# One looped TensorE program for 28 of the 32 groups, uniform window tiles, and a second stage prepared earlier

## The chip, the cores and the metric

The kernel runs on one core of one Trainium2 chip. The metric is the device time of that core in microseconds. Before the change it is 869.58 us (median of 3 runs, 869.11 to 869.75). Lower is better.

## The reference

A batch of 16 sequences with 512 tokens of 256 channels goes through two layers, each with a residual sum and a layer norm. FFT products of twice the length, cut at 512, are causal convolutions along the tokens.

```python
q = einsum('blh,dh->bdl', u, Wq) + bq ; k, v likewise          # 256 -> 256
k  = causal_conv(k_kernel, k) + k_D * k                         # one kernel of 512 taps per channel
kv = k * v
y  = (causal_conv(ssm_kernel, kv) + D * kv) * q
x  = layernorm(u + y @ Wo.T + bo)
h  = square(relu(x @ W_fc.T))                                   # 256 -> 1024
y2 = h @ W_proj.T                                               # 1024 -> 256
# five steps: mem = 0.9*mem + y2 - (mem > 1); count += mem > 1
x  = layernorm(x + count / 5)
```

## The kernel before

Every operand of TensorE is split into a high and a low 16-bit part, and three of the four products are kept, so that the sums come out nearly as in 32 bits. That is why there are so many splits: a "hi" part is a copy to 16 bits by ScalarE, a "lo" part a subtraction by GpSimd or VectorE.

**First stage (about 48 to 404 us of the span).** The 256 channels are 8 chunks of 32, and each chunk is 4 groups of 8 channels: 32 groups, numbered 0 to 31. A projection of the chunk after next is done in four quarters (four sequences each), one quarter per group. In group g TensorE does `project` (96 matmuls, for group g + 4), `conv1` of group g (96 matmuls, keys times Toeplitz windows of the first kernel) and `conv2` of group g - 1 (96 matmuls). For groups 28 to 31 there is nothing left to project. A projection fills four PSUM banks (`PA`), and the next may begin when VectorE has read them (`proj_read`).

VectorE in group g: reads the projection (keys, values, queries: L1043, L1046, L1046), multiplies conv1's result with the values (`times_v`, L1124), multiplies conv2's result of group g - 1 with the queries (`times_q`, L1130), masks and widens the second kernel's windows of g (`windows2`, L1069 and L1089), and masks the first kernel's windows of g + 2 (`windows1`, L1069; in the last four groups it also makes one of the two shifted copies, L1076). ScalarE makes the hi parts of kv and of the next group's keys (L526, L512) and widens windows (L517, L522). GpSimd makes the two lo parts (L652, L647). The chain to the next conv1 is therefore times_v, hi of kv and keys, lo of kv, lo of keys.

The windows come by DMA from a DRAM copy of the kernels, `kpad_dram`, through the queue of SyncE: 1 MB for conv1 and 0.5 MB for conv2 of each group, and up to group 23 also two `spread` DMAs that fill `kpad_dram` eight groups ahead. The tiles for conv2 lie in four different places (`slot_of`: BASE, QUERY in the tail of the queries' tile, then TOKENS and LATE), because the keys and values of two chunks are kept at once.

TensorE's program is written out for groups 0 to 2, then a loop of nine passes with two groups each runs groups 3 to 20 (L810 to L827; an If picks the code for the projection's quarter, so that a pass holds 768 matmuls and executes 576), and groups 21 to 31 are written out again. A matmul is two instructions, a weight load and the product.

**Second stage (about 436 us to the end).** For each of 16 sequences: out projection (L855), sum and layer norm, transposes (L836), up projection (L874), relu, square, split, down projection (L881), spike counts, second norm.

**Between them.** The weights of the second layer are loaded, their largest values found (L975), reduced over partitions by GpSimd (L668), and both weights are split: hi by ScalarE (L600, L601), lo by VectorE (L1183, L1186). The first sequence's y is gathered by ScalarE (L597), turned, projected out, summed (L1214), its moments taken (L1195, L1200), the root by GpSimd (L691, L694), the shift (L1206), the norm (L554), turned and split (L560, L1220), and then the first up projection can start. GpSimd meanwhile adds the bias to u (`add_bo`, L681) and gathers y of the next sequences (`gather`, L676).

## Time and profile before

| What | us |
|---|---|
| Median of 3 runs | 869.58 |
| The profiled execution: its time | 871.54 |
| Its span | 869.4 |
| TensorE busy | 744.9 |
| VectorE busy | 703.2 |
| ScalarE busy | 529.6 |
| GpSimd busy | 391.1 |
| Mean granted TensorE clock, share of full speed | 0.95 |

The profiled execution is 1.96 us above the median of the runs, and 2.1 us of it lie outside the span. A busy share over the whole span says little here: the kernel has five stretches with different limits, which the rows below keep apart. "Idle before, issue" means that an engine waited for nothing that the profile shows.

### The profile page before, as it was taken

The page shows a single profiled execution, that of the slowest core. Times are in us where ns is not written, and L with a number is a line of the kernel's source. Part 1 is how long each engine was busy: PE and PEld are TensorE (multiplying, and loading weights), DVE is VectorE, ACT ScalarE, POOL GpSimd, SP SyncE. Part 2 cuts the span into 40 slices and gives each one's busy share as a digit, 9 for nine tenths or more (in the row PEclk, how much of TensorE's full clock was granted, in tenths as well). Part 3 has the DMA queues.
Part 4 walks back from the last instruction along what each step waited for, and adds up shares of the span by engine and source line. Part 5 has one row for each costly group of instructions (what it writes and reads, how often), then busy time and mean ns, then how long its engine had stood idle before and what let it go on. Part 6 is the DMA issues. An engine that isn't in the chain of part 4 may idle for free.

```text
span 869.4 us, 26708 instructions
## 1 busy us (share of the span) xinstructions
PE 744.9 (86%) x11392; PEld 547.4 (63%) x11392; DVE 703.2 (81%) x1100; ACT 529.6 (61%) x625; POOL 391.1 (45%) x307
## 2 busy tenths in 40 slices
PE   0068879999999798775499999999999999999993
PEld 0068879999999798775355555555555455555541
DVE  6896737877878757675569999999999999999885
ACT  2383748878877757665255556665556655566661
POOL 0332212223222212221475667866668766687542
PEclk9999969999999989776699999999999999999997
DMA  9994859999999867773000110011110111101001
GB/s 336 342 245 127 198 136 215 223 232 230 221 240 229 193 156 150 156 191 99 25 25 1 49 48 25 24 48 48 48 48 0 48 48 48 48 3 47 25 25 48
DMA packets 55580, 101.01 MB, mean 116 GB/s; under 512 B 5729, under 2 KB 41441, under 8 KB 53601
## 3 DMA queue, kind: packets, MB, share of 16 engines
q1 hardware_dynamic: 54144, 97.94, 43.9%
q10 hardware_dynamic: 1376, 2.23, 0.7%
q8 instruction: 44, 0.72, 0.4%
q14 instruction: 16, 0.12, 0.1%
HBM read 89.92 MB, written 27.01 MB: 134 GB/s over the span
## 4 chain that ended last, share of the span: by engine, by line
PE 44%; DVE 21%; POOL 17%; issue 11%; ACT 4%; DMA 1%; SPq 0%; POOLq 0%; DVEq 0%; ACTq 0%
PE ps L763 18%; POOL arena L687 14%; PE ps L741 13%; DVE arena L1238 7%; PE ps L874 5%; PE ps L881 5%; DVE u_maxima L975 2%; DVE arena L1195 2%; DVE arena L1235 2%; PE ps L855 2%; DVE arena L1214 2%; DVE arena L1220 2%; ACT arena L506 1%; PE ps L836 1%; DVE arena L1206 1%
## 5 line engine op out<-in xcount | busy, mean ns | idle before, releaser
L741 PE MATMUL ps<-arena 128*128 128x96 f16 x3072 | 143.3, 210 | 62.8 <-DVE arena L1028 51.1
L687 POOL TENSOR_TENSOR arena<-arena 128x512 f16<-128x512 f32 x128 | 178.6, 1426 | 14.9 <-ACT arena L570 14.3
L741 PEld LDWEIGHTS ps<-arena 128*128 128x128 f16 x3072 | 138.4, 100 | 64.7 <-issue 58.7
L881 PE MATMUL ps<-arena 128*128 128x512 f16 x768 | 173.2, 379 | 2.7 <-POOL arena L687 2.7
L874 PE MATMUL ps<-arena 128*128 128x512 f16 x768 | 170.8, 379 | 0.9 <-issue 0.9
L763 PE MATMUL ps<-arena 128*128 128x64 f16 (+2 forms) x5088 | 148.8, 184 | 25.9 <-issue 13.3
L763 PEld LDWEIGHTS ps<-arena 128*128 128x128 f16 x5088 | 145.4, 99 | 27.8 <-issue 20.7
L652 POOL TENSOR_TENSOR arena<-arena 128x512 f16<-128x512 f32 x32 | 37.8, 1182 | 245.3 <-ACT arena L526 245.3
L1227 DVE TENSOR_TENSOR arena<-arena 128x512 f32<-128x512 f32 x128 | 138.4, 1136 | 9.6 <-POOL arena L687 7.8
L566 ACT ACTIVATE arena<-ps,read_factor 128x512 f32<-128x512 f32 x128 | 88.0, 687 | 79.4 <-PE ps L874 62.7
L881 PEld LDWEIGHTS ps<-arena 128*128 128x128 f16 x768 | 73.9, 98 | 90.4 <-POOL arena L687 9.5
L874 PEld LDWEIGHTS ps<-arena 128*128 128x128 f16 x768 | 74.4, 98 | 86.9 <-issue 1.4
L1238 DVE SCALAR_TENSOR_TENSOR arena<-ps,stair_at,arena 128x512 bf16<-128x512 f32 x128 | 96.1, 751 | 4.5
L517 ACT ACTIVATE arena<-arena 64x1792 f32<-64x1792 f32 x60 | 98.7, 1688 | 0.8
L570 ACT ACTIVATE arena<-arena 128x512 f16<-128x512 f32 x128 | 79.3, 623 | 29.3 <-DVE arena L1227 28.2
L554 ACT ACTIVATE arena<-arena 128x256 f32<-128x256 f32 x128 | 66.2, 589 | 40.0 <-DVE arena L1206 39.4
L522 ACT ACTIVATE arena<-arena 64x1792 f32<-64x1792 f32 x42 | 69.3, 1689 | 20.8 <-DVE arena L1089 20.8
L691 POOL TENSOR_TENSOR arena<-arena,eps 128x4 f32<-128x4 f32 x32 | 11.7, 364 | 141.0 <-DVE arena L1200 141.0
L1130 DVE SCALAR_TENSOR_TENSOR qy<-ps,read_factor,qy 128x512 f32<-128x512 f32 x32 | 24.0, 751 | 57.4 <-PE ps L763 57.4
L855 PE MATMUL ps<-arena 128*128 128x256 f32 x256 | 61.6, 396 | 1.2 <-ACT arena L547 1.2
L526 ACT ACTIVATE arena<-arena 128x512 f16<-128x512 f32 x32 | 20.2, 630 | 65.7 <-DVE arena L1124 65.7
L855 PEld LDWEIGHTS ps<-arena 128*128 128x128 f32 x256 | 51.2, 201 | 10.5 <-issue 1.6
(108 smaller groups left out, 901.1 us busy)
## 6 DMA issues: line engine op xcount, KB each, us to landing
arena<-kpad_dram SPq DMA_DIRECT2D x166, 256.0 KB, 5.3
kpad_dram<-ksplit_dram SPq DMA_DIRECT2D x64, 256.0 KB, 6.1
qy<-in_uT SPq DMA_DIRECT2D x8, 1024.0 KB, 17.4
arena<-in_u SPq DMA_DIRECT2D x16, 512.0 KB, 4.1
out<-arena SPq DMA_DIRECT2D x16, 512.0 KB, 3.0
qy<-kpad_dram SPq DMA_DIRECT2D x22, 256.0 KB, 6.5
arena<-in_k SPq DMA_DIRECT2D x2, 512.0 KB, 4.8
ksplit_dram<-arena ACTq DMA_DIRECT2D x2, 512.0 KB, 3.3
```

The lines of the kernel that those rows point to most:

```text
L517: nc.scalar.activation(*as_pairs(*shifted(windows1_of(s, half))), ACT.Copy).then_inc(c1_copied, 1)
L522: nc.scalar.activation(*as_pairs(*widened(windows2_of(g, half), HP)), ACT.Copy).then_inc(c2_copied, 1)
L566: nc.scalar.activation(relu_h[:, f], PH[:, f % 2], ACT.Relu, scale=read_factor[:, 4:5]).then_inc(relu_ready, 1)
L570: nc.scalar.activation(h16[:, 0, f], h_square[:, f % 4], ACT.Copy).then_inc(h_hi, 1)
L687: nc.gpsimd.tensor_tensor(h16[:, 1, f], h_square[:, f % 4], h16[:, 0, f], ALU.subtract).then_inc(h_lo, 1)
L741: last = nc.tensor.matmul(o, u16[:, x, t, tok:tok + P], wcur[:, w, t], start=(k == 0), stop=(k == 3 * DT - 1))
L763: last = nc.tensor.matmul(out[:, ch * COL + delta * B:(ch + 1) * COL], win[:, delta * P:(delta + 1) * P], data(xp, ch)[:, 0:cols], start=( ...
L855: last = nc.tensor.matmul(PW[:, j // 2, (j % 2) * D:(j % 2 + 1) * D], yT[:, t, j * P:(j + 1) * P], wo[:, t], start=(t == 0), stop=(t == DT ...
L874: last = nc.tensor.matmul(PH[:, f % 2], wf16[:, w, t, f * P:(f + 1) * P], x16[:, r, x, t], start=(k == 0), stop=(k == 3 * DT - 1))
L881: return nc.tensor.matmul(PD[:, t], wp16[:, w, f, t * P:(t + 1) * P], h16[:, h, f], start=first, stop=last)
L1227: nc.vector.tensor_tensor(h_square[:, f % 4], relu_h[:, f], relu_h[:, f], ALU.mult).then_inc(square_ready, 1)
L1238: ins = nc.vector.scalar_tensor_tensor(c, y, stair_at[:, n:n + 1], c, ALU.is_gt, ALU.add)
```

## The change

1. Keys, values and windows. The keys' and values' tiles hold one chunk instead of two: a quarter of the next chunk is written into the place that the group just used leaves free. For that the layout alternates, so that for every second chunk keys and values are read out of PSUM in four pieces of 128 columns each and not in one of 512 (`read_scaled`). The values are now read behind times_v of the same group, and with a wait for it. kv has a tile of its own. The keys' 16-bit tile has one buffer. The eight window tiles are one array `T`; all loads of conv2's windows wait for the group two before.
2. TensorE's program is written out for groups 0 to 3 and loops over groups 4 to 31 in 14 passes. A second If leaves out the projection in the last two passes.
3. End of the first stage. The second layer's weights are loaded one group earlier, u without waiting for conv2; times_q of group 30 goes behind windows2 of group 31.
4. Start of the second stage. GpSimd does both add_bo first, then both gathers, then the first root. VectorE's split of the second weight goes behind the first sequence's statistics. TensorE projects out sequence 1 before it turns x of sequence 0.

```diff
-        kbuf = part(16, F32, "p (r q n) -> p r q n", r=2, q=GPC)
-        vbuf = part(16, F32, "p (r n) -> p r n", r=2)
+        kbuf = part(8, F32, "p (a b n) -> p a b n", a=GPC, b=GPC)
+        vbuf = part(8, F32, "p (a b n) -> p a b n", a=GPC, b=GPC)
+        kv = part(2, F32)
...
-        k16 = part(4, F16, "p (r a n) -> p r a n", r=2, a=2)
+        k16 = part(2, F16, "p (a n) -> p a n", a=2)
...
-            LOOPED = range(3, QUERY_UNTIL + 1)
-            for g in range(LOOPED.start):
-                step(g)
-            with pe.Fori(0, len(LOOPED) // 2) as nth:
-                pair_of_steps(LOOPED.start, nth)
-            for g in range(LOOPED.stop, NG):
-                step(g)
+            FIRST = GPC
+            for g in range(FIRST):
+                step(g)
+            with pe.Fori(0, (NG - FIRST) // 2) as nth:
+                pair_of_steps(nth)
...
+            def read_scaled(s, buf, quarter, r, chunk, banks):
+
+                src, factor, bias_s = tiles_of(banks, s), read_factor[:, 2 * s:2 * s + 1], bias_of(chunk, s)
+                if r == 0:
+                    return nc.vector.scalar_tensor_tensor(buf[:, quarter].rearrange("p b (d m) -> p (b d) m", d=G),
+                                                          src, factor, bias_s, ALU.mult, ALU.add)
+                for n in range(GPC):
+                    some = slice(n * G, (n + 1) * G)
+                    last = nc.vector.scalar_tensor_tensor(buf[:, n, quarter].rearrange("p (d m) -> p d m", d=G),
+                                                          src[:, some], factor, bias_s[:, some], ALU.mult, ALU.add)
+                return last
...
                 if more:
-                    if s % GPC == 0 and not (first and s == 0):
-
-                        dve.wait_ge(kv_lo, g)
-                    read_projection(s % GPC, (s // GPC + 1) % 2, g + GPC, chunk + s // GPC + 1)
+                    dve.wait_ge(k_lo, g + 1)
+                    read_keys_queries(s % GPC, (s // GPC + 1) % 2, g + GPC, chunk + s // GPC + 1)
                 times_v(s, g, base + (s // GPC + 1) * GPC)
-                if g:
+                if more:
+                    dve.wait_ge(kv_ready, g + 1)
+                    read_values(s % GPC, (s // GPC + 1) % 2, chunk + s // GPC + 1)
+                if g and not (isinstance(g, int) and g == NG - 1):
                     times_q((s - 1) % PAIR, g - 1)
...
             add_bo(0, 0, 1)
+            add_bo(1, 1, 1)
             pool.wait_ge(y_ready, NG)
-            pool.wait_ge(y_seq_ready, 1)
             gather(1, 1)
+            gather(2, 0)
             root(0, 0)
-            add_bo(1, 1, 1)
-            gather(2, 0)
...
             turn_y(1, 1)
+            project_out(1)
             turn_x(0, 0)
-            pe.wait_ge(f_lo, 2)
-            pe.wait_ge(f_hi, 2)
+            pe.wait_ge(f_lo, 1)
+            pe.wait_ge(f_hi, 1)
```

VectorE in group 0, the pattern of every group of an even chunk, before: the projection is read in three instructions, then comes times_v (L1124), then windows2. Names in brackets are the semaphores that an instruction waits for.

```order
L1043 SCALAR_TENSOR_TENSOR arena<-ps,read_factor,arena 128x512 [waits proj]
L1046 TENSOR_TENSOR arena<-ps,arena 128x128x4
L1046 TENSOR_TENSOR qy<-ps,arena 128x128x4
L1124 SCALAR_TENSOR_TENSOR arena<-ps,read_factor,arena 128x512 [waits proj_read,c1_half]
L1069 TENSOR_TENSOR arena<-arena 32x8x32 [waits t2_in0]
```

The same place now, with times_v at L1076:

```order
L989 SCALAR_TENSOR_TENSOR arena<-ps,read_factor,arena 128x128 [waits proj,k_lo]
L989 SCALAR_TENSOR_TENSOR arena<-ps,read_factor,arena 128x128 x3
L998 TENSOR_TENSOR qy<-ps,arena 128x128x4
L1076 TENSOR_TENSOR arena<-ps,arena 128x4x32x4 [waits proj_read,c1_half]
L989 SCALAR_TENSOR_TENSOR arena<-ps,read_factor,arena 128x128 [waits kv_ready]
L989 SCALAR_TENSOR_TENSOR arena<-ps,read_factor,arena 128x128 x3
L1025 TENSOR_TENSOR arena<-arena 32x8x32 [waits t2_in0,t2_zero]
```

The values' reading has moved from ahead of times_v to behind it, so the projection's banks come free only after conv1, and nine instructions stand where there were three.

VectorE at the end of the first stage before, from the widening of group 30's windows on (L975 is the largest value of a weight, L1130 times_q):

```order
L1089 COPY arena<-arena 32x8x480 [waits c2_masked] x2
L975 TENSOR_REDUCE part_max<-arena 128x1 [waits ld_wf]
L1124 SCALAR_TENSOR_TENSOR arena<-ps,read_factor,arena 128x512 [waits proj_read,c1_half,vlink]
L1130 SCALAR_TENSOR_TENSOR qy<-ps,read_factor,qy 128x512 [waits c2_half]
L1069 TENSOR_TENSOR arena<-arena 32x8x32 [waits t2_in0]
L1069 TENSOR_TENSOR arena<-arena 32x8x32 [waits t2_in1]
```

The same place now (L917 is the largest value, L1083 times_q, L1025 and L1043 masks and widening):

```order
L1043 COPY arena<-arena 32x8x480 [waits c2_masked] x2
L917 TENSOR_REDUCE part_max<-arena 128x1 [waits ld_wf]
L1076 TENSOR_TENSOR arena<-ps,arena 128x4x32x4 [waits proj_read,kv_lo,c1_half,vlink]
L1025 TENSOR_TENSOR arena<-arena 32x8x32 [waits t2_in2]
L1025 TENSOR_TENSOR arena<-arena 32x8x32 [waits t2_in3]
L1043 COPY arena<-arena 32x8x480 [waits c2_masked] x2
L1083 SCALAR_TENSOR_TENSOR qy<-ps,read_factor,qy 128x512 [waits c2_half]
```

times_q of group 30 has moved behind the masks and the widening of group 31.

GpSimd between the stages before, from the reduction over partitions on (L681 is add_bo, L676 gather, L691 and L694 the root):

```order
L668 ISA all_max<-part_max 128x3 [waits part_max2_done]
L681 ISA
L681 TENSOR_TENSOR arena<-arena 128x1024 [waits ld_u_seq0,ld_wo]
L676 COPY arena<-qy 128x1024 [waits y_seq_ready,y_ready]
L691 TENSOR_TENSOR arena<-arena,eps 128x4 [waits moments1_ready]
L694 TENSOR_TENSOR arena<-arena,half_neg 128x4 [waits var_eps_ready0]
L681 TENSOR_TENSOR arena<-arena 128x1024 [waits ld_u_seq1]
L676 COPY arena<-qy 128x1024 [waits y_turned]
```

And now:

```order
L611 ISA all_max<-part_max 128x3 [waits part_max2_done]
L624 ISA
L624 TENSOR_TENSOR arena<-arena 128x1024 [waits ld_u_seq0,ld_wo]
L624 TENSOR_TENSOR arena<-arena 128x1024 [waits ld_u_seq1]
L619 COPY arena<-qy 128x1024 [waits y_ready]
L619 COPY arena<-qy 128x1024 [waits y_turned]
L634 TENSOR_TENSOR arena<-arena,eps 128x4 [waits moments1_ready]
L637 TENSOR_TENSOR arena<-arena,half_neg 128x4 [waits var_eps_ready0]
```

The second add_bo and the second gather now stand ahead of the first root.

## Rows read from the trace of the kernel before

**Rows 1.** Busy time by stretch: length, then each engine (instructions), clock, DMA share, GB/s.
```profile
101.60:131.30 29.70, 22.30 (x582) 21.74 (x577) 14.44 (x24) 16.31 (x13) 5.66 (x6) 0.77 0.66 151
131.30:279.30 148.00, 146.62 (x4609) 145.99 (x4610) 116.94 (x180) 120.78 (x94) 36.34 (x31) 1.00 0.99 227
279.30:359.10 79.80, 69.74 (x2021) 68.44 (x2017) 54.21 (x82) 55.91 (x45) 17.79 (x15) 0.94 0.72 161
359.10:403.90 44.80, 29.49 (x865) 28.52 (x864) 33.05 (x44) 26.75 (x21) 9.76 (x9) 0.70 0.75 188
...
435.50:869.40 433.90, 415.71 (x2121) 225.12 (x2119) 389.43 (x644) 250.02 (x409) 282.53 (x217) 0.99 0.11 35
```

**Rows 2.** Timeline of TensorE, groups 21 and 22: start, length, line, instructions, idle before.
```profile
287.83 2.28 PE L763 MATMUL ps<-arena 128*128 128x64 f16 x82 [1.44 <-issue]
289.96 2.12 PE L741 MATMUL ps<-arena 128*128 128x96 f16 x46
292.94 2.29 PE L741 MATMUL ps<-arena 128*128 128x96 f16 x50 [0.86 <-issue]
```

**Rows 3.** DMA queues in the looped stretch 131.3 to 279.3 us: packets, MB, share.
```profile
q14 instruction: 4, 0.03, 0.1%
```

**Rows 4.** DMA queues in the written-out stretch 279.3 to 359.1 us.
```profile
q8 instruction: 15, 0.25, 1.4%
```

**Rows 5.** Timeline of VectorE in one looped group.
```profile
210.05 0.74 DVE L1043 SCALAR_TENSOR_TENSOR arena<-ps,read_factor,arena 128x512 f32<-128x512 f32 x1
...
212.31 0.75 DVE L1124 SCALAR_TENSOR_TENSOR arena<-ps,read_factor,arena 128x512 f32<-128x512 f32 x1 [0.34 <-PE ps L763]
214.82 0.75 DVE L1130 SCALAR_TENSOR_TENSOR qy<-ps,read_factor,qy 128x512 f32<-128x512 f32 x1 [1.75 <-PE ps L763]
```

**Rows 6.** Timeline of all engines, same group: the next projection, and GpSimd's lo part.
```profile
213.81 1.16 POOL L652 TENSOR_TENSOR arena<-arena 128x512 f16<-128x512 f32 x1 [7.11 <-ACT arena L526]
...
214.64 4.24 PE L741 MATMUL ps<-arena 128*128 128x96 f16 x96
```

**Rows 7.** Timeline of VectorE near the start: a 256-column instruction.
```profile
42.65 0.35 DVE L1021 TENSOR_SCALAR arena<-arena,d_scale 128x256 f32<-128x256 f32 x1
```

**Rows 8.** Timeline of TensorE, group 1: the wait ahead of its convolutions.
```profile
85.91 5.17 PE L763 MATMUL ps<-arena 128*128 128x64 f16 x192 [1.48 <-POOL arena L647]
```

**Rows 9.** Timeline of all engines, groups 28 to 31.
```profile
367.64 6.58 PE L763 MATMUL ps<-arena 128*128 128x32 f16 x185 [3.28 <-issue]
...
371.06 0.75 DVE L1130 SCALAR_TENSOR_TENSOR qy<-ps,read_factor,qy 128x512 f32<-128x512 f32 x1 [4.05 <-PE ps L763]
...
372.23 2.22 DVE L1089 COPY arena<-arena 32x3840 f16<-32x3840 f16 x2
...
373.41 3.29 ACT L522 ACTIVATE arena<-arena 64x1792 f32<-64x1792 f32 x2 [3.50 <-DVE arena L1089]
...
391.13 2.29 DVE L975 TENSOR_REDUCE part_max<-arena 128x1 f32<-128x2048 f32 x1
...
394.95 1.16 POOL L652 TENSOR_TENSOR arena<-arena 128x512 f16<-128x512 f32 x1 [6.44 <-ACT arena L526]
```

**Rows 10.** Timeline of all engines, between the stages.
```profile
403.90 0.38 POOL L668 PARTITION_ALL_REDUCE all_max<-part_max  x1 [7.80 <-issue]
...
411.11 2.34 POOL L681 TENSOR_TENSOR arena<-arena 128x1024 f32<-128x1024 f32 x1 [6.83 <-issue]
...
423.96 2.31 DVE L1206 SCALAR_TENSOR_TENSOR arena<-arena 128x4 f32<-128x4 f32 x1 [1.46 <-POOL arena L694]
426.19 1.92 POOL L676 COPY arena<-qy 128x1024 f32<-128x1024 f32 x1
...
428.43 1.97 PE L836 MATMUL ps<-ident,arena 128*128 128x128 f32 x8 [9.93 <-ACT arena L554]
430.19 5.51 PE L855 MATMUL ps<-arena 128*128 128x256 f32 x16
...
435.54 10.52 PE L874 MATMUL ps<-arena 128*128 128x512 f16 x48
```

More of the change, by code:

```diff
@@ L415, in _ @@
                     spread(s + AHEAD)
-                second = [(g, half) for g in range(1, NG) for half in range(2) if loaded_at(g, half) == s]
-                for g, half in second:
-                    if not use_before(g, half) and slot_of(g, half)[0] != LATE:
-                        load_windows2(g, half)
                 if s + 2 < NG:
@@ L783, in conv1 @@
                     pe.wait_ge(kv_ready, g - 1)
-                convolve(0, PC1[:, s % 2], lambda a, ch: k16[:, s % 2, a, ch * COL:(ch + 1) * COL],
-                         lambda half, c, a: windows1_of(s, half)[:, c, a], g + 1, c1_half)
+                for half in range(2):
+                    pe.wait_ge(c1_copied[half], g + 1)
+                    convolve(half, PC1[:, s % 2], k16, lambda c, a: windows1_of(s, half)[:, c, a], c1_half)
             def conv2(s, g):
@@ L914, in body @@
             def body(i, r, left):
-                if left:
+                if left and not (isinstance(i, int) and i == 0):
                     project_out(i + 1)
@@ L1050, in read_projection, with read_values @@
+            def read_values(quarter, r, chunk, banks=PA):
+                read_scaled(1, vbuf, quarter, r, chunk, banks).then_inc(proj_read, 1)
                 if quarter == GPC - 1 and chunk + 1 < NC:
@@ L1053, in read_projection @@
                     nc.vector.tensor_copy(wcur, wnext).then_inc(wcur_ready, 2)
+            def read_projection(quarter, r, n, chunk, banks=PA):
+                read_keys_queries(quarter, r, n, chunk, banks)
+                read_values(quarter, r, chunk, banks)
             def mask(conv, s, g, half):
@@ L1059, in mask @@
                 else:
-                    place, nth = slot_of(g, half)
-                    times = USES[place, nth].index((g, half)) + 1
-                    dve.wait_ge(t2_in[2 * place + nth], 16 * times * (PIECES if place == TOKENS else 1))
+                    dve.wait_ge(t2_in[s % 2 * 2 + half], 8 * (g - s % 2) + 16)
                 if conv:
```

295 lines of the change are left out of this document (121 added, 174 removed).

## Prediction

> **What bounds the kernel now.** I read the busy time by stretch first, because the page's shares over the whole span mix five stretches [rows 1]. From 435.5 us on TensorE is busy for 415.7 of 433.9 us and the granted clock is 0.99: the second stage is one long TensorE stretch that the change leaves alone. Whatever makes it start earlier is handed to the end in full. From 131.3 to 279.3 us TensorE is busy for 146.6 of 148.0 us at full clock. These are 16 looped groups, 9.25 us each. TensorE is the bound, and VectorE with 116.9 us has 1.9 us of air in a group. From 279.3 to 359.1 us the same 288 matmuls a group take 79.8 / 7 = 11.4 us, though VectorE and the DMA queues are less busy than before (DMA share 0.72 against 0.99). So no engine's work is the bound there.
>
> The timeline of TensorE shows what is: gaps that nothing in the profile releases, put down to "issue". One lies ahead of 287.83, the next ahead of 292.94, and between them stand 82 + 46 = 128 matmuls [rows 2], which are 256 instructions. The same distance returns all along the written-out groups. The DMA queues say why this is code: in the written-out stretch the queue marked instruction moved 15 packets with 0.25 MB [rows 4], 16.7 KB a packet, and 7 x 288 matmuls make 15.75 pieces of 128: one packet for each 128 matmuls. In the looped stretch there is no row of that queue at all; what is marked instruction there is another queue with 0.03 MB [rows 3]. A loop body that is in place is not loaded again; straight code is loaded block by block and TensorE waits at block boundaries. The first pass of the loop, 101.6 to 131.3 us, took 29.7 us for the work of 18.5, at clock 0.77 [rows 1]. That is the price of loading a body.
>
> The Trainium skill, "Runtime: NRT & Kernel Launch", section "Instruction fetch mechanics", has two rules on this. It says that crossing a 16 KiB boundary is mostly hidden; the trace disagrees, with 1.44 and 0.86 us in front of two neighbouring blocks [rows 2]. By that rule the written-out groups would gain nothing from a loop. It also says that a taken branch out of the two-page window forces a fetch and that kernels prefer to be unrolled; the eight passes of rows 1 and 3 speak against it here. Both are rivals below, with times worked out from rows.
>
> **The change, part by part.** All sums are on the profiled execution, 871.54 us, which is 1.96 above the median of the runs.
>
> Start, group 0. The values are now read behind times_v, so the projection of group 1 waits for conv1 of group 0, then times_v (0.75) and the values. In even chunks these are four pieces of 128 columns. No row shows such a piece; it lies between a quarter of the 0.74 us of the 512-column one [rows 5], 0.19 us, and the 0.35 us of a 256-column instruction [rows 7]. I take 0.30, nearer to the second, whose width is the nearer one, and keep 0.35 for the bound. So 0.75 + 0.1 for the wait + 1.2 = 2.05 us later. Of this 1.48 was waited for GpSimd anyway, ahead of conv1 of group 1 [rows 8]. The rest with the later key chain: **+0.8**.
>
> Groups 4 to 27, VectorE in the looped group. Before, reading starts at 210.05 and times_v at 212.31 with 0.34 us idle; then VectorE idles 1.75 us until conv2 is done, and TensorE starts the next projection at 214.64 [rows 5, 6]. Now keys (4 x 0.30) and queries (at most 0.74) end at 212.0, times_v still runs from 212.31 to 213.06, the values end at 213.06 + 0.1 + 1.2 = 214.4. That is 0.25 us before TensorE wants the banks. At 0.35 a piece it is 214.56, still in time; the cover is the 1.75 us of idle time, and it is then used up. If a piece costs 0.45 each of the 16 groups with pieces (12 of them looped) waits some 0.35 us. I take **0**, and +5 as the end of the bound. The one key buffer costs nothing: hi of the keys is made behind times_v, thus behind conv1 in any case. SyncE's loads keep the order that groups 1 to 19 have now, and there the DMA share is 0.99 and TensorE does not wait.
>
> The Trainium skill, "VectorE: DVE Perf Modes", section "The TRN2 errata", gives a fixed price per instruction and advises tiles of 512 elements or more, against this change. By its formula of 58 to 120 cycles beside 128 columns a piece is an estimated 0.19 to 0.26 us; no run here shows one yet, and with it the sum stays at 0.
>
> Group 3 is written out now, at 11.4 instead of 9.25 us: **+2.1**. The loop's first pass moves from groups 3 and 4 to 4 and 5 and costs what it cost.
>
> Groups 21 to 27 at the looped pace: 79.8 - 7 x 9.25 = **-15.0**. So group 27 ends at 359.1 - 15.0 + 2.9 = 347.0.
>
> Groups 28 to 31, 359.1 to 403.9. Here a cycle runs over three engines: times_q at 371.06, masks, widening from 372.23 (half of 2.22 for the first half of the channels), ScalarE's two copies (3.29), and the second half of conv2, about a quarter of the 6.58 us for two convolutions at low clock [rows 9]: 1.17 + 1.11 + 3.29 + 1.65 with 0.4 for hand-overs = 7.6 us from times_q to times_q. Group 28 took 12.0 (359.1 to 371.06) because of a code stall of 3.28 us ahead of 367.64 and the copies behind it. New: times_q of 27, 28 and 29 come 7.8 us apart, 23.4 us after the start. Then 0.75, masks and widening 3.2, the largest value 2.29 [rows 9], times_v of group 31 with 0.75, and kv's lo part ends 1.91 us after times_v does (213.06 to 213.81 + 1.16 [rows 5, 6]): 32.3 us, with some tenths for the low clock 32.6. Before it ended at 396.11, that is 37.0 us after the start. **-4.4**. times_q of group 31 then follows some 5 us later instead of 7.8, but it isn't what is late next.
>
> Between the stages GpSimd is. Its reduction needs a code load: it starts 7.80 us after kv's lo part, and add_bo another 7.2 us after that, at 411.11, with 6.83 us idle [rows 10]. That is 15.0 us behind kv's lo part, and I keep it. Before, root of sequence 0 ended when the shift began, 423.96, 27.85 behind it. The shift waited for VectorE's second split. Now that split stands behind the shift, and GpSimd does 2 x 2.34 (add_bo) + 2 x 1.92 (gather without VectorE's split beside it [rows 10]) and then the root, 0.2 + 1.1: 15.0 + 4.7 + 3.9 + 1.3 = 24.9. **-2.9**. The two splits' order alone would have given 4; GpSimd's order takes a part of it back. The shift took 2.31 us beside GpSimd's add_bo for 4 columns; now nothing runs beside it, 0.2: **-2.1**. The moved split (up to 4 us, beside a busy GpSimd) lies under norm, transposes and hi part.
>
> From the end of the norm to the first up projection: 428.4 to 435.54 is 7.1 us, with transposes, hi and lo part, and the out projection of sequence 1, 5.51 us at low clock, in front [rows 10]. Now it waits only for the out projection that began before (0 to 2 us), then transposes 1.0 to 2.0, hi 1.0, lo 1.2: 3.4 to 6.4. I take 5.0: **-2.1**.
>
> Sum: 0.8 + 0 + 2.1 - 15.0 - 4.4 - 2.9 - 2.1 - 2.1 = -23.6. Profiled 847.9, median **846.0 us**.
>
> **Rivals.**
>
> A, the values' reading becomes TensorE's wait. For it: 0.25 us of cover. Against it: the bound of 0.35 us a piece. With +5 us: 851.
>
> B, the gain between the stages is eaten, because GpSimd's code load, its two add_bo and a slower clock set the first root. 7.1 us of the sum go: 853.
>
> C, the gaps aren't loading of code (the first rule above) but go with the state of the end, for instance its tiles' loads. Then groups 21 to 27 keep their 11.4 us: 846.0 + 15.0 = 861. Against it: the 128-matmul distance.
>
> D, slower: the second rule above, as a mechanism here. The body no longer stays in place, because a second If is added, and each pass loads it. The first pass shows the price, 29.7 - 18.5 = 11.2 us; 13 further passes make +146 us and the time 992. It decides when the body exceeds what is kept: now it is again 768 matmuls with a few compare instructions more. Eight passes of the old body cost nothing, so the margin must be smaller than those few instructions.
>
> **How the numbers follow.** The forecast 0.74, A 0.09, B 0.09, C 0.04, D 0.04. Its own range is 841 to 851: clock and hand-overs in groups 28 to 31 and between the stages are worth some 4 us to each side. The range for 8 in 10 reaches over A and B and to a tail in which the clock rises: 839 to 856. A measurement of this kernel can tell 0.2%, 1.7 us, from no change. Faster 0.95 (forecast, A, B, C and a rest), same 0.01, slower 0.04.
>
> **What would show it.** TensorE's groups 4 to 27 in pairs of 18.5 us from the second pass on, without packets in the second instruction queue; 29 to 30 us for the first pass. No idle time of TensorE released by VectorE's reading. Group 27's end near 347 us, kv's lo part of group 31 near 379.5, the root near 404.5, the first up projection near 412, and from there 434 us to the end. The forecast is wrong if the passes are longer than 18.7 us, if pieces take over 0.35 us, or if the first up projection starts after 418.

## The result

| | median us | runs | range |
|---|---|---|---|
| before, beside it | 869.66 | 4 | 869.11 to 871.72 |
| changed | 859.80 | 4 | 858.63 to 861.3 |

The ratio is 0.9878, 95% interval 0.9852 to 0.9903: 9.9 us faster, where the forecast had 23.6 and a range of 839 to 856. The sign was right and the size was not. The profiled execution took 861.3 us, its span is 859.3. Measured once more beside the later experiments, the changed kernel gave 860.62 (858.76 to 861.44, 4 runs, 868.91 for the kernel before), with a second profile.

### The profile page after: what moved, and what is told of

Its sections match the earlier page's. It is cut to its first block, busy times and chain, and to the rows that moved or that the text cites. A ratio compares the mean times of both kernels' runs of the same rounds, so it can differ in the third digit from the quotient of the medians.

```text
span 859.3 us, 26944 instructions
## 1 busy us (share of the span) xinstructions
PE 743.8 (87%) x11392; PEld 545.7 (64%) x11392; DVE 713.3 (83%) x1192; ACT 529.9 (62%) x625; POOL 390.3 (45%) x307
## 4 chain that ended last, share of the span: by engine, by line
PE 44%; DVE 24%; POOL 17%; issue 10%; DMA 2%; ACT 1%; SPq 0%; POOLq 0%; DVEq 0%; ACTq 0%
PE ps L697 16%; PE ps L683 15%; POOL arena L630 14%; DVE arena L1184 7%; PE ps L813 5%; PE ps L820 5%; DVE u_maxima L917 2%; DVE arena L1181 2%; PE ps L794 2%; DVE arena L1141 2%; DVE arena L1166 2%; DVE arena L1160 2%; DVE arena L971 1%; DMA arena<-kpad_dram 1%; PE ps L772 1%
## 5 line engine op out<-in xcount | busy, mean ns | idle before, releaser
L697 PE MATMUL ps<-arena 128*128 128x64 f16 (+3 forms) x6144 | 172.2, 182 | 23.3 <-issue 8.9
L697 PEld LDWEIGHTS ps<-arena 128*128 128x128 f16 x6144 | 169.7, 97 | 24.5 <-issue 14.7
L683 PEld LDWEIGHTS ps<-arena 128*128 128x128 f16 x3072 | 138.4, 101 | 64.6 <-issue 56.4
L820 PEld LDWEIGHTS ps<-arena 128*128 128x128 f16 x768 | 74.0, 98 | 90.6 <-POOL arena L630 9.7
L813 PEld LDWEIGHTS ps<-arena 128*128 128x128 f16 x768 | 74.3, 98 | 89.5 <-issue 4.0
L467 ACT ACTIVATE arena<-arena 64x1792 f32<-64x1792 f32 x64 | 105.1, 1687 | 14.7 <-DVE arena L1043 14.7
L462 ACT ACTIVATE arena<-arena 64x1792 f32<-64x1792 f32 x60 | 98.7, 1689 | 0.8
L514 ACT ACTIVATE arena<-arena 128x512 f16<-128x512 f32 x128 | 79.3, 623 | 29.4 <-DVE arena L1173 28.4
L1043 DVE COPY arena<-arena 32x3840 f16<-32x3840 f16 x64 | 72.9, 1177 | 1.0
L1025 DVE TENSOR_TENSOR arena<-arena 64x512 f16<-64x512 f16 (+1 forms) x128 | 58.3, 482 | 10.6 <-DMA arena<-kpad_dram 9.6
L794 PE MATMUL ps<-arena 128*128 128x256 f32 x256 | 64.0, 407 | 2.3 <-ACT arena L491 2.3
L794 PEld LDWEIGHTS ps<-arena 128*128 128x128 f32 x256 | 52.7, 207 | 12.6 <-issue 1.6
```

Of the source, the lines that this page charges most:

```text
L462: nc.scalar.activation(*as_pairs(*shifted(windows1_of(s, half))), ACT.Copy).then_inc(c1_copied[half], 1)
L467: nc.scalar.activation(*as_pairs(*widened(windows2_of(g, half), HP)), ACT.Copy).then_inc(c2_copied, 1)
L514: nc.scalar.activation(h16[:, 0, f], h_square[:, f % 4], ACT.Copy).then_inc(h_hi, 1)
L683: last = nc.tensor.matmul(o, u16[:, x, t, tok:tok + P], wcur[:, w, t], start=(k == 0), stop=(k == 3 * DT - 1))
L697: last = nc.tensor.matmul(out[:, ch * COL + delta * B:(ch + 1) * COL], taps(c, tp)[:, delta * P:(delta + 1) * P], data[:, xp, ch * COL:ch ...
L794: last = nc.tensor.matmul(PW[:, j // 2, (j % 2) * D:(j % 2 + 1) * D], yT[:, t, j * P:(j + 1) * P], wo[:, t], start=(t == 0), stop=(t == DT ...
```

## The profile after

Busy time by stretch of the changed kernel, with the columns of [rows 1]: group 3; the first pass of the loop; the eleven passes over groups 6 to 27; groups 28 to 31; between the stages; second stage.
```profile
104.00:116.00 12.00, 11.09 (x295) 10.73 (x291) 8.74 (x19) 7.21 (x7) 2.42 (x3) 0.87 0.73 164
116.00:146.80 30.80, 21.58 (x577) 21.13 (x577) 14.37 (x23) 16.38 (x13) 5.25 (x5) 0.83 0.66 150
146.80:354.20 207.40, 202.78 (x6336) 201.26 (x6336) 173.96 (x320) 168.06 (x131) 51.27 (x44) 1.00 0.94 213
354.20:395.60 41.40, 27.05 (x865) 26.37 (x864) 35.69 (x43) 28.03 (x22) 11.23 (x9) 0.86 0.82 199
395.60:425.25 29.65, 18.12 (x56) 14.25 (x57) 11.91 (x30) 10.85 (x10) 11.19 (x7) 0.62 0.06 18
425.25:859.30 434.05, 415.62 (x2120) 225.11 (x2120) 388.55 (x644) 250.07 (x409) 283.05 (x217) 0.99 0.11 35
```
The second stage is what it was, 434.05 against 433.9 us. Everything lies in when it starts: 425.25 against 435.54 before and about 412 forecast. The seven groups that took 11.4 us each now run at the loop's pace, and the queue that had 15 packets there [rows 4] is gone from the whole looped stretch; only the other instruction queue is left:
```profile
q1 hardware_dynamic: 19425, 44.15, 94.2%
q14 instruction: 5, 0.04, 0.1%
```
But a pass takes 207.4 / 11 = 18.85 us, not 18.5 (from the first projection of one pass to that of the next it is 18.89 over the ten passes from 146.79 to 335.71). In TensorE's timeline (columns as in [rows 2]) the first projections of four successive passes stand behind gaps, three of them released by nothing and one by VectorE's copy of the chunk's weights (L1007):
```profile
165.74 4.25 PE L683 MATMUL ps<-arena 128*128 128x96 f16 x96 [0.43 <-issue]
...
184.60 4.25 PE L683 MATMUL ps<-arena 128*128 128x96 f16 x96 [0.50 <-issue]
...
203.53 1.66 PE L683 MATMUL ps<-arena 128*128 128x96 f16 x35 [0.42 <-DVE arena L1007]
...
222.36 4.25 PE L683 MATMUL ps<-arena 128*128 128x96 f16 x96 [0.46 <-issue]
```
VectorE in the same kernel, near the end of the loop and in groups 29 and 30: two pieces of 128 columns (L989) take 0.60 us, 0.30 each as forecast. In group 29 VectorE waits 2.06 us for windows from memory, and its widening for group 30 takes 3.18 us instead of 2.22:
```profile
353.74 0.60 DVE L989 SCALAR_TENSOR_TENSOR arena<-ps,read_factor,arena 128x128 f32<-128x128 f32 x2
...
375.34 0.42 DVE L1025 TENSOR_TENSOR arena<-arena 64x512 f16<-64x512 f16 x1
377.82 0.42 DVE L1025 TENSOR_TENSOR arena<-arena 64x512 f16<-64x512 f16 x1 [2.06 <-DMA arena<-kpad_dram]
...
382.15 3.18 DVE L1043 COPY arena<-arena 32x3840 f16<-32x3840 f16 x2
```
Between the stages, TensorE and then GpSimd. The out projection of sequence 1 (the second L794) starts at 415.24, behind GpSimd's gather, and holds the transposes of x until 421.75, though ScalarE's norm had begun at 415.54 and ended at 417.62:
```profile
412.15 1.97 PE L772 MATMUL ps<-ident,arena 128*128 128x128 f32 x8 [3.90 <-POOL arena L619]
415.24 6.68 PE L794 MATMUL ps<-arena 128*128 128x256 f32 x16 [1.11 <-ACT arena L491]
421.75 1.04 PE L772 MATMUL ps<-ident,arena 128*128 128x128 f32 x8
425.25 7.07 PE L813 MATMUL ps<-arena 128*128 128x512 f16 x32 [2.46 <-DVE arena L1166]
```
```profile
396.90 0.39 POOL L611 PARTITION_ALL_REDUCE all_max<-part_max  x1 [5.94 <-issue]
404.43 5.81 POOL L624 TENSOR_TENSOR arena<-arena 128x1024 f32<-128x1024 f32 x2 [7.15 <-issue]
410.20 3.81 POOL L619 COPY arena<-qy 128x1024 f32<-128x1024 f32 x2
413.98 0.19 POOL L634 TENSOR_TENSOR arena<-arena,eps 128x4 f32<-128x4 f32 x1
414.25 1.06 POOL L637 TENSOR_TENSOR arena<-arena,half_neg 128x4 f32<-128x4 f32 x1
```

## The experiments

All start from the changed kernel. The kernel before was measured beside every group of them and had medians of 868.91 to 870.25 us. Single profiles are compared by what happens inside them. The start of the first stage alone shifts a whole profile by up to 3 us: with the same code ahead of it, group 3 starts at 101.80 where the granted clock from 72 us on was 0.94, and at 104.92 where it was 0.84.

### Is it the loading of code?

Groups 4 to 31 written out.
```
-            with pe.Fori(0, (NG - FIRST) // 2) as nth:
-                pair_of_steps(nth)
+            for g in range(FIRST, NG):
+                step(g)
```


> The changed kernel with TensorE's groups 4 to 31 written out, no loop and no branch. Theory (code is loaded block by block and TensorE waits at block boundaries): no pace of 9.25 us anywhere, groups 6 to 27 at about 11.4 us each instead of the 9.44 of the changed kernel, so group 27 ends some 43 us later, near 397 us of the span, about 150 packets of 16 KB in the second instruction queue over the first stage, total near 895 to 905 us. Rival (the gaps belong to the state at the stage's end, not to code): groups at 9.25 us, since the branches are gone too, total near 855 us.

Measured: 898.97 us (one run), 39 us more than the loop. The written-out program's instruction queue over the whole span:
```profile
q8 instruction: 79, 1.29, 0.7%
```
against 25 packets and 0.41 MB in the changed kernel. That is half of the 150 packets that had been expected, a miscount: 28 groups of 288 matmuls make 63 pieces of 128. TensorE in one of these groups, with 81 + 47 = 128 matmuls between two gaps:
```profile
220.34 3.60 PE L683 MATMUL ps<-arena 128*128 128x96 f16 x81 [2.01 <-issue]
223.78 1.38 PE L697 MATMUL ps<-arena 128*128 128x64 f16 x47
226.65 3.49 PE L697 MATMUL ps<-arena 128*128 128x16 f16 x127 [1.50 <-issue]
```
Groups 6 to 27 take 11.3 us each (138.88 to 386.85), and group 27 ends 10 us earlier than expected. The same tile places and transfers, only TensorE's program differs, and the gaps are back all along it. So rival C of the prediction falls: the gaps are loading of code.

The Trainium skill, "Runtime: NRT & Kernel Launch", section "Instruction fetch mechanics", calls the crossing of a 16 KiB boundary mostly hidden; this run disagrees, by 39 us.

Four groups in one pass, which needs no If, in six passes, with groups 28 to 31 written out.
```
-            with pe.Fori(0, (NG - FIRST) // 2) as nth:
-                pair_of_steps(nth)
+            with pe.Fori(0, (NG - GPC - FIRST) // GPC) as nth:
+                four_steps(nth)
+            for g in range(NG - GPC, NG):
+                step(g)
```


> The changed kernel with a loop of 6 passes of four groups (groups 4 to 27) and no If at all: a pass holds 1152 matmuls instead of 768. Groups 28 to 31 are written out. Theory (a body stays in place only up to some size between 768 and 1152 matmuls, and is loaded in every pass beyond it): groups at 11 to 12 us in every pass, packets in the second instruction queue throughout, total near 900 us. Rival (any loop stays in place): four groups in 37.0 us, that is 9.25 each, no packets after the first pass, total near 856 us.

Measured: 920.5 us (one run), the slowest of all. Its queue, and the start of one of its passes:
```profile
q8 instruction: 88, 1.44, 0.7%
```
```profile
215.11 6.73 PE L683 MATMUL ps<-arena 128*128 128x96 f16 x96 [6.46 <-issue]
```
A body of 1152 matmuls is loaded again in every pass, with 4.8 to 6.5 us ahead of it and 50 to 51 us for four groups, which is worse than straight code. The body of 768 matmuls stays in place. The mechanism of rival D exists; its threshold lies between the two and the change is on the good side.

The same section of the Trainium skill says that a taken branch out of the two-page window forces a fetch. Two pages of 16 KiB are too few for the changed kernel, whose body of 768 matmuls is 6 blocks and drew no packet in eleven passes. But the section also gives TensorE a larger memory than the other engines, 128 KiB or 2048 instructions, and with that both runs agree: 1536 instructions stay, 2304 don't.

### Why 18.9 us a pass?

The outer If of each projection taken away, groups 28 to 31 written out.
```
-                with pe.If(nth < (NG - GPC - FIRST) // 2):
-                    with pe.If(nth % 2 == 0):
+                with pe.If(nth % 2 == 0):
...
-            with pe.Fori(0, (NG - FIRST) // 2) as nth:
+            with pe.Fori(0, (NG - GPC - FIRST) // 2) as nth:
                 pair_of_steps(nth)
+            for g in range(NG - GPC, NG):
+                step(g)
```


> The changed kernel with the loop over groups 4 to 27 only (12 passes) and without the second If; groups 28 to 31 are written out. Theory (each further branch of a pass costs some 0.2 us of TensorE's time): passes of 18.5 us again instead of 18.89, so the start of group 28 comes 4.3 us earlier, near 350 us; behind it the written-out groups show issue gaps again, which may take back 1 to 3 us; total near 857 us. Rival (the passes are longer because of VectorE's later reading of the values or of the transfers): passes stay at 18.9 us, the start of group 28 stays at 354 us, total 860 to 862 us.

Measured: 860.82 (859.34 to 861.93, 5 runs). The passes take 18.62 us, 0.27 less, as the theory had it, and group 28 starts near 350.7 instead of 354.2. But the last four groups, written out again, lose nearly the same (30 packets of code against 25, and 74.1 us from there to the first up projection instead of 71.05), so the time is where the rival had it.

The loop over groups 3 to 26 as in the kernel before, with one If and the uniform places.
```
-            FIRST = GPC
+            FIRST = 3
...
-            with pe.Fori(0, (NG - FIRST) // 2) as nth:
-                pair_of_steps(nth)
+            with pe.Fori(0, 12) as nth:
+                pair_of_steps(nth)
+            for g in range(FIRST + 24, NG):
+                step(g)
```


> The tile places and all engines but TensorE as changed; TensorE's program is groups 0 to 2 written out, a loop of 12 passes over groups 3 to 26 with one If ahead of each projection as in the kernel before, and groups 27 to 31 written out. Theory: the second pair of Ifs costs 0.25 us a pass in groups 4 to 27, and writing out group 3 costs 2.7 us; so passes take 18.6 us and the loop's first pass begins at 104 (not 116); the group-27 part is written out again, 2 to 3 us more, and the tail's code stalls cost what they cost in the kernel with one If (about 3 us against the loop). Group 28 starts near 352 and the time is 858 to 861. Rival: the slower passes come from VectorE's order and the smaller pieces, then passes take 18.9 us as in the changed kernel and the time is 862 to 865.

Measured: 856.19 (856.1 to 859.26, 4 runs), 2 us better than the theory had. Ten passes from 132.03 to 318.50 make 18.65 us each. Group 28 starts near 347.6, 6.6 us earlier than in the changed kernel: 2.3 of these lie ahead of group 3 (101.72 against 104.01), where both have the same code and the clock differs (0.94 against 0.89), 3.4 in groups 3 to 5 (39.4 against 42.8 us), the rest behind them, where the written-out group 27 gives some of the passes' gain back. Groups 28 to 31 and the time between the stages cost 72.5 against 71.05 us: their code stalls give back 1.5.

Two Ifs more, around the first convolutions.
```
+                with pe.If(nth < NG):
-                conv1(0, g)
+                    conv1(0, g)
```


> The changed kernel with two more Ifs in TensorE's loop body, one around conv1 of each group, whose condition always holds; no matmul is added. Theory: each If that TensorE passes at a boundary of a group costs it some 0.12 to 0.25 us of waiting that nothing releases. The passes grow from 18.89 by 0.25 to 0.5 us to 19.1 to 19.4, and the time from 859.8 by 14 x 0.25 to 14 x 0.5 to 863 to 867. Rival: the longer passes come from VectorE's smaller pieces and its order, or from the If ahead of a projection waiting for the reading: passes stay at 18.9 us and the time at 860.

Measured: 861.61 (860.88 to 862.17, 4 runs) against 860.62 for the changed kernel beside it, passes of 18.91 us against 18.90. Nothing gained on the question: a condition that always holds is dropped when the program is built, so TensorE's program has 10 unconditional jumps instead of 8 and the same 6 comparing branches. The two jumps add nothing that shows, here in front of the first convolutions.

The same around the projections.
```
+                with pe.If(nth < NG):
                     with pe.If(nth < (NG - GPC - FIRST) // 2):
```


> The changed kernel with a third If around each of the two projections of TensorE's loop body, whose condition always holds. Two more Ifs around the first convolutions left the passes at 18.9 us. Theory: what costs is an If in front of a projection, where the loop's jump and the other Ifs stand already: taking one level away gave 0.24 to 0.27 us a pass, so one more level adds as much: passes of 19.1 to 19.2 us and 863 to 864. Rival: an If costs nothing anywhere as long as the body stays in place, and the 0.25 us come from something else that went with it (how the two branches lie in the code): 18.9 us and 860.

Measured: 860.64 (859.09 to 861.01, 4 runs), passes of 18.89. For the same reason this was the changed kernel once more, with the same 8 jumps and 6 comparing branches, and it told nothing for either side.

Then with a condition that has to be compared.
```
+                with pe.If(nth < (NG - FIRST) // 2 - 1):
                     with pe.If(nth < (NG - GPC - FIRST) // 2):
```


> The changed kernel with a third If around each of the two projections, now with a condition that TensorE has to compare itself (it holds in the first 13 of 14 passes); the Ifs with a condition that always held had been dropped when the program was built, so they had added no comparison at all. Theory: a comparison with its branch in front of a projection costs TensorE 0.12 to 0.25 us each, since one level less gave 0.24 to 0.27 us a pass: passes grow from 18.89 to 19.1 to 19.4, the time to 863 to 866. Rival: the branch as such is free and the difference came with something else: passes of 18.9 us, 860.

> As the kernel with the third compared If, but only around the second projection of the body, away from the loop's jump back. Theory: both places cost the same, so passes grow by half of what both together do (19.0 to 19.15). Rival: only the place behind the loop's jump costs, then passes of 18.9 us here and all of the growth belongs to the first.

Measured: both places 863.07 (860.11 to 865.67, 5 runs), the second place alone 860.19 (2 runs). The timeline of TensorE tells more than the times. Two passes of the first:
```profile
299.25 4.25 PE L683 MATMUL ps<-arena 128*128 128x96 f16 x96 [0.63 <-issue]
308.63 4.25 PE L683 MATMUL ps<-arena 128*128 128x96 f16 x96
318.43 4.25 PE L683 MATMUL ps<-arena 128*128 128x96 f16 x96 [0.55 <-issue]
327.67 4.25 PE L683 MATMUL ps<-arena 128*128 128x96 f16 x96
337.49 4.25 PE L683 MATMUL ps<-arena 128*128 128x96 f16 x96 [0.58 <-issue]
```
and of the second:
```profile
298.69 4.25 PE L683 MATMUL ps<-arena 128*128 128x96 f16 x96 [0.46 <-issue]
308.07 4.25 PE L683 MATMUL ps<-arena 128*128 128x96 f16 x96
317.75 4.25 PE L683 MATMUL ps<-arena 128*128 128x96 f16 x96 [0.43 <-issue]
327.02 4.25 PE L683 MATMUL ps<-arena 128*128 128x96 f16 x96
336.73 4.25 PE L683 MATMUL ps<-arena 128*128 128x96 f16 x96 [0.46 <-issue]
```
From 146.04 to 337.49 are ten passes: 19.145 us each, 0.25 more. From 146.61 to 336.73: 19.01, 0.12 more. So a compared branch in front of a projection costs TensorE 0.12 us, at the second place by this run and at the first by the difference of the two, and the two Ifs that the change adds are 0.25 us of the 0.35 to 0.4 that a pass is longer.

The rest, some 0.1 us a pass, stays open. The row with L1007 above is a candidate: once in four passes TensorE waits for the copy of the weights, which now stands behind the values' reading. In the kernel looped from group 3 that wait has a price. It comes ahead of the second projection, and the pass around it takes 19.13 us where the others take 18.47 to 18.65:
```profile
187.58 4.25 PE L683 MATMUL ps<-arena 128*128 128x96 f16 x96
197.20 4.25 PE L683 MATMUL ps<-arena 128*128 128x96 f16 x96 [0.37 <-DVE arena L1007]
206.71 4.25 PE L683 MATMUL ps<-arena 128*128 128x96 f16 x96 [0.26 <-issue]
```
That is 0.5 us in four passes, 0.12 a pass. In the changed kernel the same wait adds nothing: two successive passes take 37.76 and 37.80 us with it and 37.76 to 37.81 without, since a gap of the same length stands there in any case. So rival A, that the reading and what follows it make TensorE wait, did not cost the changed kernel time, and where it shows it is about 1.5 us in 12 passes, not 5.

### Groups 28 to 31

The loads of the second stage's weights one group later each, where they were before.
```
-                if s == NG - 4:
+                if s == NG - 3:
                     sp.dma_start(wf_st, ...).then_inc(ld_wf, 16)
-                if s == NG - 3:
+                if s == NG - 2:
                     sp.dma_start(wp_st, ...).then_inc(ld_wp, 16)
```


> The changed kernel with the second layer's two weights loaded one group later, where they were before. Theory (the 1 MB load of the first weight goes ahead of group 31's windows and delays them): VectorE's wait of 2.06 us for windows ahead of times_v of group 30 is gone, kv's lo part of group 31 ends some 2 us earlier relative to the start of group 28, total 857.5 to 859 us. Rival (the windows come late anyway, or the later weight delays the largest value instead): the total does not move by more than 0.5 us, or it is slower by up to 1 us.

Measured: 858.61 (857.15 to 861.22, 4 runs). The medians of 858.61 and 859.8 (860.62 later) can't be told apart, the profiles can. VectorE in groups 29 and 30: no wait for windows, and the widening is back at 2.22:
```profile
374.14 0.75 DVE L1025 TENSOR_TENSOR arena<-arena 64x512 f16<-64x512 f16 x2
...
380.24 2.22 DVE L1043 COPY arena<-arena 32x3840 f16<-32x3840 f16 x2
```
The stretch from the start of group 28 to the first up projection is 68.35 us against 71.05, 2.7 less. Of these 1.7 lie ahead of the end of kv's lo part of group 31 (35.05 us after the start against 36.8, and 36.8 again in the second profile of the changed kernel). The rest lies between the stages, where profiles of the same code differ by as much (next section), so 1.7 is what the loads show.

### Between the stages

The out projection of sequence 1 put back behind the transposes.
```
-                if left and not (isinstance(i, int) and i == 0):
+                if left:
                     project_out(i + 1)
...
             turn_y(1, 1)
-            project_out(1)
             turn_x(0, 0)
```


> The out projection of sequence 1 is put back behind the transposes of x (before the first up projection), the rest as changed. Theory: in the changed kernel it started only at 415.24, since y of sequence 1 is gathered at the earliest behind two add_bo, and its 6.68 us at low clock held the transposes until 421.75, though the norm was done at 417.62. Put back, the transposes start at 417.7 (after the norm), hi and lo part are done by 421.1, but the projection then runs from 418.7 to 425.4 and the first up projection starts at 425.4: 0 to +0.5 us against the changed kernel, 859.8 to 860.5. The move of this projection by itself bought nothing. Rival (the forecast's view, the order of the two is worth 2.1 us): the up projection starts near 427.5 and the time is 862.

Measured: 858.48 (858.11 to 860.13, 4 runs). From the reduction (L611) to the first up projection 424.13 - 395.99 = 28.1 us against 28.35. Moving it bought nothing. The spread of this stretch is worth knowing: the ten other profiles whose code between the stages is that of the changed kernel have 26.9 to 28.3, most of them 27.8 or more.

GpSimd's order.
```
             add_bo(0, 0, 1)
-            add_bo(1, 1, 1)
             pool.wait_ge(y_ready, NG)
             gather(1, 1)
-            gather(2, 0)
+            add_bo(1, 1, 1)
             root(0, 0)
+            gather(2, 0)
```


> GpSimd does add_bo(0), gather(1), add_bo(1), root(0), gather(2) in place of add_bo(0), add_bo(1), gather(1), gather(2), root(0). Theory: what holds the first up projection back is the start of the out projection of sequence 1, and that waits for gather(1). gather(1) now ends near 409.3 instead of 412.1, the out projection runs from 412.4 to 419.1, the root ends at 413.4, the norm near 416, the transposes start at 419.1 and the first up projection near 422.5: 2.7 us earlier than 425.25, 857.1. Rival: the norm or the splits set the start and the order of GpSimd is worth nothing: 859.8.

Measured: 857.14 (855.33 to 859.0, 4 runs), as the theory had it. TensorE:
```profile
410.85 1.93 PE L772 MATMUL ps<-ident,arena 128*128 128x128 f32 x8 [2.13 <-POOL arena L619]
413.89 5.62 PE L794 MATMUL ps<-arena 128*128 128x256 f32 x16 [1.11 <-ACT arena L491]
419.35 1.04 PE L772 MATMUL ps<-ident,arena 128*128 128x128 f32 x8
422.85 9.44 PE L813 MATMUL ps<-arena 128*128 128x512 f16 x43 [2.47 <-DVE arena L1166]
```
From the reduction at 397.64 to the up projection are 25.2 us, 3.1 less than in the changed kernel. The two further kernels with this order, below, have 24.8 and 25.6, so all three lie under the whole spread of the old order, by 1.4 us at the least.

The second layer's split put back in front of the first sum.
```
+            dve.wait_ge(f_hi, 2)
+            nc.vector.scalar_tensor_tensor(wp16[:, 1], wp_st, ...).then_inc(f_lo, 1)
...
             first_sum(0, 0)
             norm_shift(0, 0)
-            dve.wait_ge(f_hi, 2)
-            nc.vector.scalar_tensor_tensor(wp16[:, 1], wp_st, ...).then_inc(f_lo, 1)
```


> VectorE's split of the second layer's weights is put back ahead of the first sum, the rest as changed. Theory: the first split ended at 405.72 and the first sum waited until 408.29 for the out projection, so the second split (2.35 us alone) fits into that idle time: the sum starts at 408.3 to 409.5 (the split runs beside GpSimd's add_bo and may take up to 4 us), GpSimd's add_bo get up to 1 us longer, and the root, which stands behind two gathers, ends 0 to 1 us later: 859.8 to 861. Rival (the forecast's view, that putting the split behind the statistics is worth 4 us of which GpSimd's order takes a part back): root and up projection come 2 to 4 us later, 862 to 864.

Measured: 861.95 (861.48 to 863.89, 4 runs). GpSimd's two add_bo and VectorE's second split:
```profile
403.84 8.14 POOL L624 TENSOR_TENSOR arena<-arena 128x1024 f32<-128x1024 f32 x2 [6.83 <-issue]
```
```profile
405.34 4.43 DVE L1135 SCALAR_TENSOR_TENSOR arena<-arena,w_scale 128x2048 f16<-128x2048 f32 x1
```
The split takes 4.43 us beside add_bo instead of 2.35, and the two add_bo 8.14 instead of 5.81. From the reduction to the up projection 29.0 us, 0.7 more. The median is 1.3 to 2.2 above the changed kernel, so the time is on the edge between the two theories; the profile speaks for the smaller price. The new place of the split was right by a small amount, and what it frees is GpSimd.

### Together

Late loads and GpSimd's order on the changed loop.

> The changed kernel with the later loads of wf and wp and GpSimd's order add_bo(0), gather(1), add_bo(1), root(0), gather(2). The loop is the changed one. If the two causes are independent: times_q of group 31 comes 2.7 us earlier after the start of group 28 and the first up projection 7.2 instead of 7.6 us behind the norm with the norm itself earlier: 859.8 - 2.7 - 2.4 = 854.7, by the medians 856.0. Rival: they share one wait, then 857.1, what the better of them has alone.

Measured: 854.59 (853.25 to 855.36, 4 runs), where the sum had 854.7 and the rival 857.1. From the start of group 28 to the first up projection are 66.7 us, against 68.35 with the late loads, 68.2 with GpSimd's order, and 71.05 and 70.65 in the two profiles of the changed kernel. So the two add up for the most part. The times alone don't prove it: as ratios to the kernel before they are 0.9834 (0.9807 to 0.9861) for both edits and 0.9841 (0.9812 to 0.987) for GpSimd's order alone.

All three: the loop over groups 3 to 26, late loads, GpSimd's order.

> Three edits on the changed kernel together: TensorE's loop over groups 3 to 26 with one If a projection and groups 27 to 31 written out, the loads of wf and wp one group later each (as in the kernel before), and GpSimd's order add_bo(0), gather(1), add_bo(1), root(0), gather(2). If the three causes add up: 859.8 - 3.6 - 1.2 - 2.7 = 852.3, by the profiles of each (-5.3, -2.7 and -2.4 at the first up projection) 849.5. Rival: in the written-out groups 27 to 31 the stalls of TensorE that nothing releases set the pace, so the later loads give nothing there: 854.

Measured: 852.95 (852.27 to 855.7, 5 runs), ratio to before 0.9823 (0.9799 to 0.9847), against 860.62 for the changed kernel beside it: 7.7 us faster. The sum of the three (852.3) and the rival (854) both lie within the range of its runs, so this doesn't decide between them, and its runs overlap with those of the two edits above. It has the lowest median found.

## Why the prediction was wrong

The end of each step, on the profiled execution of the changed kernel; the miss is 861.3 - 847.9 = 13.4 us.

| step | forecast | measured | miss |
|---|---|---|---|
| start of group 3 | 102.4 | 104.01 | +1.6 |
| groups 3 to 5 | 40.9 | 42.8 | +1.9 |
| 11 passes, groups 6 to 27 | 203.5 | 207.4 | +3.9 |
| start of 28 to kv's lo part of 31 | 32.6 | 36.8 | +4.2 |
| lo part to root | 24.9 | 24.35 | -0.6 |
| root to first up | 7.3 | 9.94 | +2.6 |

**Right.** The central reading, that the gaps are code loading at every 128 matmuls and a body in place is free of them. Rivals C and D fall with it. Also about 0.30 us a piece (the Trainium skill's formula, "VectorE: DVE Perf Modes", section "The TRN2 errata", gave an estimated 0.19 to 0.26), and the shift at 0.16 us without GpSimd beside it. Rival B, that the gain between the stages is eaten, did not come: from kv's lo part to the first up projection are 34.3 us instead of 39.4, 5.1 of the 7.1 forecast.

**Right by luck.** The stretch from kv's lo part to the root: -2.9 forecast, -3.5 measured. The forecast kept 15.0 us from kv's lo part to add_bo, on the ground that the reduction needs a code load behind the lo part. It was 13.5. The reduction waits for VectorE's last largest value (the semaphore `part_max2_done`). VectorE finds it here, before and now, and has the small product of it behind, done at 402.08 and 395.19:
```profile
399.55 2.29 DVE L975 TENSOR_REDUCE part_max<-arena 128x1 f32<-128x2048 f32 x1
```
```profile
392.67 2.27 DVE L917 TENSOR_REDUCE part_max<-arena 128x1 f32<-128x2048 f32 x1
```
The reduction starts 1.8 us behind that before, 1.7 now, and 1.5 to 2.1 in the profiles of the experiments. Before, the value came 6.0 us behind kv's lo part, now 4.2, since times_q of group 30 no longer makes VectorE wait ahead of the masks. The forecast had no term for this part of the change. Against it stand the two add_bo, 5.81 instead of 4.7 beside VectorE's first split.

**Groups 4 to 27 at 0** is the step that failed most: 3.9 us over the eleven passes and 1.1 in the first (30.8 against 29.7). It held the extra compare instructions for nothing in time and weighed them only as code size (rival D). Shown: 0.12 us for each, twice a pass, which is 2.8 of the 3.9 us; the other 1.1 and the first pass stay open. The prediction checked that the values' reading ends before TensorE wants the banks, and left out the copy of the weights that follows it on VectorE at the end of each chunk. TensorE does wait for that copy, but in the changed kernel at no price.

**Groups 28 to 31 at -4.4** gave -0.2 by kv's lo part. The model had the cycle of times_q, masks, widening, copies and conv2, 7.8 us. Measured, times_q of 27 comes 8.7 us after the stretch begins (conv1 of 28 waits 2.65 us for ScalarE's copy of its windows; in ScalarE's order that copy stands behind the keys' hi part, which waits for the values' reading), that of 28 another 7.9 and that of 29 another 9.2 (8.5 with the late loads), since windows stood behind a megabyte of weights in the queue. The change puts these loads one group earlier, and the forecast gave that no term. The late loads show 1.7 us of the miss. The 2.65 us wait was not tried alone. From times_q of 29 to the end of kv's lo part of 31 are 11.0 us instead of 9.2, mostly because the widening of group 30 took 3.18 instead of 2.22 and the lo part, which now runs beside the widening of group 31, 1.84 instead of 1.16.

**Norm to first up at 5.0** was 7.6. It gave the out projection of sequence 1, already begun, 0 to 2 us ahead of the transposes. That projection started only 2.4 us before the norm's end, because gather(1) stands behind two add_bo, took 6.68 us instead of 5.51, and held the transposes for 4.1. Both orders of TensorE cost the same (28.1 and 28.35). GpSimd's order alone gives 3.1, or 1.4 at the least by the spread above.

**Start and group 3.** The start moved 0.1 to 3.3 us in the profiles. Where TensorE's projections 0 and 1 ran at 5.85 us instead of 4.25 (granted clock 0.89 for that stretch) it is 2.4; in the kernel from group 3 on, with 4.25 for the first, group 3 starts at 101.72, 0.1 late. So this term is within the clock of a run. Group 3 written out and then the first pass cost 42.0 to 43.2 us in the profiles with the changed loop, where the loop from group 3 takes 39.4 for the same three groups: 2.6 to 3.8 against 2.1.

The range was too narrow because five of the six misses have one sign: where the rows left a choice, most terms took the better side, and the sum added these.

## What to carry to other kernels

A loop is worth having where code is loaded block by block, but its body must fit: here 768 matmuls stay in place and 1152 do not, and too large a body is worse than straight code. Branches that compare, in front of TensorE's work, are not free where TensorE is the bound (here busy for 202.78 of 207.40 us): count them. Before an idle stretch is kept as a fixed price, look up which semaphore the instruction waits for. When an engine does a row of small jobs in a gap between stages, sort them by who waits next (here gather(1) ahead of the second add_bo, some 3 us), and keep large loads behind the small ones of the current stage.

## What had not been expected of the hardware

- A compared branch ahead of a projection: 0.12 us of TensorE each; two unconditional jumps in the body, ahead of convolutions: nothing measurable (passes of 18.91 against 18.90 us).
- VectorE's split of 128 x 2048 takes 2.35 us alone and 4.43 beside GpSimd's add_bo, and two add_bo 5.8 or 8.1 us. Side by side little is saved: with both splits beside them the work spans 403.07 to 411.98 us, 8.9, and one after the other the four would take 9.4. VectorE's widening and GpSimd's lo part do the same, 3.17 and 1.84 us together where each alone takes 2.22 and 1.16.
- A body that doesn't stay in place costs 4.8 to 6.5 us at the head of each pass and further gaps inside, 50 to 51 us for 37 us of work.
